# The norms' variances and shifts one element at a time, with a scalar pointer

## The chip, the cores and the metric

The kernel runs on one core of a Trainium2 chip. The metric is the device time of one execution in microseconds, the median of the runs taken. Five engines work side by side, each with its own list of instructions, and meet through semaphores: TensorE (PE, the matmuls), VectorE (DVE), ScalarE (ACT, activations), GpSimd (POOL) and SyncE (SP, which issues the DMAs).

## What is computed

The input is x, 8 x 512 rows of 256 floats. Two blocks follow each other, each added to its input:

```python
def _layernorm(x, axis=-1, eps=1e-05):
    m = jnp.mean(x, axis=axis, keepdims=True)
    v = jnp.var(x, axis=axis, keepdims=True)
    return (x - m) / jnp.sqrt(v + eps)
...
x = x + attn_ref(_layernorm(x))   # norm, linear attention (F = 64), norm, 256 -> 1024 -> 256 with GELU
x = x + ffn_ref(_layernorm(x))    # ternary weights, 256 -> 1024, GELU, norm over 1024, 1024 -> 256
```

`attn_ref` normalises its input, forms Q = elu(..)+1 and K = elu(..)+1 (64 features) and V (256), runs causal linear attention along the sequence with a denominator, applies the output projection and a residual, normalises again and runs an MLP with exact GELU and a residual. `ffn_ref` multiplies by weights rounded to -1, 0, 1 about their mean absolute value, applies GELU, a norm with weight and bias over 1024, and a second ternary matmul. Everything is float32.

## The kernel before

The 4096 rows are worked in 8 groups g of 512 rows, each as T = 4 tiles t of 128 rows on the partitions; h = 0, 1 names a half, two tiles. Float32 products are made as three passes of a faster type on a high and a low part (`split3`, L178 to L180), so that each operand is first written as `_hi` by ACT and then as `_lo` by DVE (`lo_part`, L806).

The order of the work is written out by hand. Each engine has a function `first` for the start, a function `step(g)` for g = 1 to 5, and `last`; they call the pieces of work of several groups in turn, so that a step holds the MLPs of group g, the end of group g-1 and the attention of group g+1. An engine does its list in order; `wait_ge` on a semaphore holds it, and everything behind it on that engine, until the count is reached.

There are four norms. For each of them DVE takes statistics (`bn_stats`), writes one element to a scratch tile (`fence`, L770), aggregates to mean and variance per row (`bn_aggr` to `mv`, L772), writes `ve` = variance + eps (`variance`, L779), POOL raises it to -1/2 (`rs`, L1043, and L1036 for the first norm), and DVE writes `sh` = -mean x rs (`shift`, L784). Norms 1 to 3 (n = 0, 1, 2) are then applied by ACT as scale and bias of an activation (`normalise`, L503): norm 1 of x gives u (for Q, K, V) and n1, the residual; norm 2 gives z, which PE transposes (L186) and ACT and DVE split into z2T; norm 3 gives z3T in the same way. Norm 4 is applied after the last matmul: `correct` (L930) adds csum x sh, and `output` (L947) multiplies by rs.

The first norm is two norms in one: `_layernorm` and then the attention's own one. Its `ve` and `sh` have two rows of four elements (L794, L795, L802); norms 2 to 4 work on the two elements of a half. Where each of them stands among DVE's pieces of work can be read in `first`, `step` and `last`.

POOL adds, besides its powers: n1 + bo (`n1o`, L1061), x + f2b (`xpb`, L1073), y + xa (`xs`, L1080) and y + cpj (`y_cpj`, L1090), each as two tensor_tensor operations of 128x512, one for each half.

The functions that the change touches, and what calls them:

Of the kernel before, what the change touches and what calls it, by code (L numbers as in the profile page):

```python
# [7 lines left out]
ALU = mybir.AluOpType  # L8
# [4 lines left out]
LN_EPS = 1e-5  # L13
# [6 lines left out]
def build(nc, x, wqk_d, wv_d, wo_d, f1_d, f2_d, fc_d, pj_d, vec_d, rows_d, out):  # L20
    G, N, D = x.shape
    FQ = 64
    T = N // P
# [11 lines left out]
    with ExitStack() as ctx:  # L35
        def sb(name, shape, dt=F32):
            return ctx.enter_context(nc.sbuf_tensor(name, shape, dt))

        def sem(name):
            return ctx.enter_context(nc.semaphore(name))  # L40
# [64 lines left out]
        mv = [sb(f"mv{n}", [P, T, 2]) for n in range(4)]  # L105
        ve = [sb("ve0", [P, 2, T])] + [sb(f"ve{n}", [P, T]) for n in (1, 2, 3)]
        rs = [sb("rs0", [P, 2, T])] + [sb(f"rs{n}", [P, T]) for n in (1, 2, 3)]
        sh = [sb("sh0", [P, 2, T])] + [sb(f"sh{n}", [P, T]) for n in (1, 2, 3)]
# [25 lines left out]
        s = {n: sem(n) for n in names}  # L134
# [309 lines left out]
        def _(act):  # L444
# [56 lines left out]
            def normalise(dst, src, n, t, row, ready):  # L501
                bias, scale = [a[n][:, row, t:t + 1] if n == 0 else a[n][:, t:t + 1] for a in (sh, rs)]
                act.activation(dst[:, t, :], src[:, t, :], ACT.Identity, bias=bias, scale=scale).then_inc(s[ready], 1)  # L503

            def u_norm(g, h):
                act.wait_ge(s["ln1_sh"], 2 * g + 1)
                if g:
                    act.wait_ge(s["tu_done"], 2 * (g - 1) + h + 1)
                for t in (2 * h, 2 * h + 1):
                    normalise(u, x_sb, 0, t, 1, "u_ready")  # L510

            def n1(g):
                act.wait_ge(s["ln1_sh"], 2 * g + 2)
                if g:
                    act.wait_ge(s["z2_ready"], 4 * g)
                    act.wait_ge(s["xs_ready"], 2 * g)
                else:
                    act.wait_ge(s["bvo_done"], 1)
                for t in range(T):
                    normalise(xa, x_sb, 0, t, 0, "n1_ready")  # L520
# [42 lines left out]
                act.activation(v[0][:, 2 * h:2 * h + 2, 0:D], by_k(bank_a[h]), ACT.Copy).then_inc(s["v_hi"], 1)  # L563

            def z2_norm(g, h):
                act.wait_ge(s["ln2_sh"], 2 * g + h + 1)
                if g:
                    act.wait_ge(s["tz3_done"], 2 * (g - 1) + h + 1)
                for t in (2 * h, 2 * h + 1):
                    normalise(z, xa, 1, t, 0, "z2_ready")  # L570
# [18 lines left out]
                act.activation(hr[0][:, (8 * g + m) % RH, :], bank_f[m % 2][:], ACT.Copy).then_inc(s["h_hi"], 1)  # L589

            def z3_norm(g, h):
                act.wait_ge(s["ln3_sh"], 2 * g + h + 1)
                act.wait_ge(s["tz2_done"], 2 * g + h + 1)
                for t in (2 * h, 2 * h + 1):
                    normalise(z, y, 2, t, 0, "z3_ready")
# [26 lines left out]
            def first():  # L622

                ln3_hi(); u_norm(0, 0); wqk_hi(); u_norm(0, 1); u_hi(0, 0); u_hi(0, 1); wvo_hi(); wf1_hi(0)
                wf1_hi(1); qk_exp(0); wf1_hi(2); qk_hi(0); eps_split(); wf2_hi(0); n1(0); ae_hi(0); ad_hi(0)
                wf2_hi(1); wf1_hi(3); af_hi(0); wf2_hi(2); v_hi(0, 0); wf2_hi(3); v_hi(0, 1); abs_part(0)
                abs_part(1); abs_part(2); abs_part(3); z2_norm(0, 0); z2_norm(0, 1); z2_hi(0, 0); z2_hi(0, 1)
                u_norm(1, 0); gelu(0, 0); h_hi(0, 0); gelu(0, 1); u_hi(1, 0); u_norm(1, 1); h_hi(0, 1); gelu(0, 2)
                u_hi(1, 1); n1(1); h_hi(0, 2); gelu(0, 3); h_hi(0, 3); qk_exp(1); gelu(0, 4); h_hi(0, 4); qk_hi(1)
                rows(); gelu(0, 5); h_hi(0, 5); gelu(0, 6); h_hi(0, 6); af_hi(1); gelu(0, 7); h_hi(0, 7)  # L630
                spread_copy(); ad_hi(1); ae_hi(1); v_hi(1, 0); v_hi(1, 1); z3_norm(0, 0); z3_norm(0, 1); z3_hi(0, 0)
                z3_hi(0, 1); gelu3(0, 0, 0); gelu3(0, 0, 1); gelu3(0, 1, 0); z2_norm(1, 0); gelu3(0, 1, 1)
                gelu3(0, 2, 0); g_hi(0, 0, 0); gelu3(0, 2, 1); g_hi(0, 0, 1); z2_norm(1, 1); g_hi(0, 0, 2)
                gelu3(0, 3, 0); z2_hi(1, 0); z2_hi(1, 1); g_hi(0, 0, 3); gelu3(0, 3, 1); u_norm(2, 0)
# [34 lines left out]
        def _(dve):  # L669
# [97 lines left out]
            def aggregate(n, ts, bn_count, mv_count):  # L767

                dve.wait_ge(s[f"ln{n + 1}_bn"], bn_count)
                dve.tensor_scalar(fence[:], neg_half[:, 0:1], 1.0, None, ALU.mult)  # L770
                for t in ts:
                    dve.bn_aggr(mv[n][:, t, :], bn[n][:, t, :]).then_inc(s[f"ln{n + 1}_mv"], 1)  # L772
                dve.wait_ge(s[f"ln{n + 1}_mv"], mv_count)

            def variance(n, g, h):

                if g:
                    dve.wait_ge(s[f"ln{n + 1}_rs"], 2 * (g - 1) + h + 1)
                dve.tensor_scalar(ve[n][:, 2 * h:2 * h + 2], mv[n][:, 2 * h:2 * h + 2, 1], 1.0, LN_EPS,  # L779
                                  ALU.mult, ALU.add).then_inc(s[f"ln{n + 1}_ve"], 1)  # L780

            def shift(n, g, h):
                dve.wait_ge(s[f"ln{n + 1}_rs"], 2 * g + h + 1)
                dve.scalar_tensor_tensor(sh[n][:, 2 * h:2 * h + 2], mv[n][:, 2 * h:2 * h + 2, 0], -1.0,  # L784
                                         rs[n][:, 2 * h:2 * h + 2], ALU.mult, ALU.mult).then_inc(s[f"ln{n + 1}_sh"], 1)

            def ln1_stats(g):
                for t in range(T):
                    dve.wait_ge(s[f"x_loaded{t // 2}"], 16 * g + 16)
                    dve.bn_stats(bn[0][:, t, :], x_sb[:, t, :]).then_inc(s["ln1_bn"], 1)  # L790
                aggregate(0, range(T), 4 * g + 4, 4 * g + 4)
                if g:
                    dve.wait_ge(s["ln1_rs"], g)
                dve.tensor_scalar(ve[0][:, 0, :], mv[0][:, :, 1], 1.0, LN_EPS, ALU.mult, ALU.add).then_inc(s["ln1_ve"], 1)  # L794
                dve.tensor_scalar(ve[0][:, 1, :], mv[0][:, :, 1], 1.0 + LN_EPS, LN_EPS * LN_EPS,  # L795
                                  ALU.mult, ALU.add).then_inc(s["ln1_ve"], 1)

            def ln1_shift(g):

                dve.wait_ge(s["ln1_rs"], g + 1)  # L800
                for row in (1, 0):
                    dve.scalar_tensor_tensor(sh[0][:, row, :], mv[0][:, :, 0], -1.0, rs[0][:, row, :],  # L802
                                             ALU.mult, ALU.mult).then_inc(s["ln1_sh"], 1)

            def lo_part(dst, b, hi, ready):
                dve.tensor_tensor(dst, b, hi.bitcast(F32), ALU.subtract).then_inc(s[ready], 1)  # L806
# [70 lines left out]
            def ln2_var(g, h):  # L877
                aggregate(1, (2 * h, 2 * h + 1), 4 * g + 2 * h + 2, 4 * g + 2 * h + 2)
                variance(1, g, h)
# [20 lines left out]
            def ln3_stats(g, h):  # L900
                dve.wait_ge(s["y_ready"], 2 * g + h + 1)
                for t in (2 * h, 2 * h + 1):
                    dve.bn_stats(bn[2][:, t, :], y[:, t, :]).then_inc(s["ln3_bn"], 1)
                aggregate(2, (2 * h, 2 * h + 1), 4 * g + 2 * h + 2, 4 * g + 2 * h + 2)
                variance(2, g, h)
# [18 lines left out]
            def correct(g, h):  # L924

                shift(3, g, h)
                dve.wait_ge(s["ln4_sh"], 2 * g + h + 1)
                dve.wait_ge(s["yc_ready"], 2 * g + h + 1)
                for t in (2 * h, 2 * h + 1):
                    dve.scalar_tensor_tensor(yc[:, t, :], csum_b, sh[3][:, t:t + 1], yc[:, t, :],  # L930
                                             ALU.mult, ALU.add).then_inc(s["corrected"], 1)
# [76 lines left out]
        def _(pool):  # L1008
# [18 lines left out]
                return row.unsqueeze(1).to_broadcast([P, 2, D])  # L1027

            def ln1_rstd(g):
                pool.wait_ge(s["ln1_ve"], 2 * g + 2)  # L1030
                if g:
                    pool.wait_ge(s["u_ready"], 4 * g)
                    pool.wait_ge(s["n1_ready"], 4 * g)
                else:
                    pool.wait_ge(s["sums_w"], 1)
                pool.tensor_tensor(rs[0][:].rearrange("p c t -> p (c t)"), ve[0][:].rearrange("p c t -> p (c t)"),  # L1036
                                   neg_half[:], ALU.pow).then_inc(s["ln1_rs"], 1)

            def rstd(n, g, h, freed, count):
                pool.wait_ge(s[f"ln{n + 1}_ve"], 2 * g + h + 1)  # L1040
                if g:
                    pool.wait_ge(s[freed], count)
                pool.tensor_tensor(rs[n][:, 2 * h:2 * h + 2], ve[n][:, 2 * h:2 * h + 2], neg_half[:, 0:2],  # L1043
                                   ALU.pow).then_inc(s[f"ln{n + 1}_rs"], 1)
# [113 lines left out]
```

## Time and profile before

| | us |
|---|---|
| median of 3 runs | 482.81 (481.68 to 483.86) |
| the profiled execution | 483.59 |
| its span | 481.8 |
| mean granted TensorE clock, share of full | 0.971 |
| PE busy, share of the span | 455.1, 94% |
| DVE busy | 385.3, 80% |
| ACT busy | 324.1, 67% |
| POOL busy | 134.4, 28% |

The span goes from the first to the last instruction of the program; the execution's own time is 1.8 us longer. Busy time is the union of an engine's instructions. A group of instructions is shown by line, engine, operation, the tile that it writes and those it reads, with its count, its busy time, the mean of one in ns, and the idle time of the engine ahead of it with what ended that idle time. Instructions of one engine overlap in the records, so that the next can start before the one ahead has ended; what an instruction costs its engine is read from start to start.

### The profile page before, as it was taken

To read this page: it belongs to the slowest core of one execution; us is meant where nothing else is said; L and a number is where in the kernel's file an instruction comes from. 1 tells how busy PE (TensorE), PEld (TensorE's weight loads), DVE (VectorE), ACT (ScalarE), POOL (GpSimd) and SP (SyncE) were. 2 spreads that over 40 slices of the span, in tenths; PEclk is the share of its full clock that TensorE was granted. 3 is DMA by queue.
4 is the path that set the end of the run, shared out by engine and by line. 5 is a ranking of instruction groups with operands and counts; after the bars stand their busy time and mean duration, and the time that the engine had idled before them with its cause. 6 is when DMAs were issued, how large, how long until landed. Compare 5 with 4: busy or idle time off the path is not lost.

```text
span 481.8 us, 8668 instructions
## 1 busy us (share of the span) xinstructions
PE 455.1 (94%) x3010; PEld 409.9 (85%) x3010; DVE 385.3 (80%) x1011; ACT 324.1 (67%) x611; POOL 134.4 (28%) x132
## 2 busy tenths in 40 slices
PE   4786998999999999999999999999999989999796
PEld 4785888889988899889988899889989889889686
DVE  4686969886997969976997969976999688874767
ACT  3776864797558783897558783897469854783263
POOL 2173305310372023600371023600361021501400
PEclk9875999999999999999999999999999999999889
DMA  8330000100020000100010000100020000000001
GB/s 252 131 114 19 1 0 1 44 23 2 0 68 1 24 0 24 45 22 1 3 65 1 23 1 24 45 22 1 2 66 2 24 0 23 1 23 2 22 0 45
DMA packets 10042, 14.06 MB, mean 29 GB/s; under 512 B 784, under 2 KB 9104, under 8 KB 9488
## 3 DMA queue, kind: packets, MB, share of 16 engines
q1 hardware_dynamic: 10000, 13.52, 8.3%
q8 instruction: 24, 0.39, 0.4%
q14 instruction: 18, 0.15, 0.1%
HBM read 9.32 MB, written 4.19 MB: 28 GB/s over the span
## 4 chain that ended last, share of the span: by engine, by line
PE 64%; DVE 17%; issue 11%; ACT 2%; POOL 2%; DMA 1%; SPq 0%; DVEq 0%; POOLq 0%; ACTq 0%
PE bank_p L393 8%; PE bank_y L178 6%; PE bank_f L363 6%; PE bank_y L179 6%; PE bank_y L180 6%; PE bank_f L178 6%; PE bank_f L179 5%; PE bank_f L180 5%; PE bank_y L377 4%; PE bank_a L186 3%; DVE sh L784 2%; DVE bn L918 2%; PE bank_a L178 2%; PE bank_a L180 2%; PE bank_a L179 2%
## 5 line engine op out<-in xcount | busy, mean ns | idle before, releaser
L1043 POOL TENSOR_TENSOR rs<-ve,neg_half 128x2 f32<-128x2 f32 x48 | 33.6, 702 | 245.9 <-DVE ve L779 245.9
L178 PE MATMUL bank_y<-wf_hi,h_hi 128*128 128x256 f32 x256 | 72.4, 283 | 1.5 <-DVE h_lo L806 1.5
L179 PE MATMUL bank_y<-wf_lo,h_hi 128*128 128x256 f32 x256 | 71.5, 279 | 0.0
L180 PE MATMUL bank_y<-wf_hi,h_lo 128*128 128x256 f32 x256 | 71.5, 279 | 0.0
L806 DVE TENSOR_TENSOR h_lo<-bank_f,h_hi 128x512 fp32r<-128x512 f32 x64 | 43.9, 686 | 28.4 <-ACT h_hi L589 28.2
L393 PE MATMUL bank_p<-wpj_t,g_hi 128*128 128x256 f32 x256 | 65.1, 289 | 0.4 <-DVE g_lo L938 0.2
L393 PE MATMUL bank_p<-wpj_t,g_lo 128*128 128x256 f32 x256 | 62.6, 280 | 0.0
L938 DVE SCALAR_TENSOR_TENSOR g_lo<-bank_y,vec,g_hi 128x256 fp32r<-128x256 f32 x128 | 54.9, 475 | 6.5 <-ACT g_hi L619 6.3
L619 ACT ACTIVATE g_hi<-bank_y,vec 128x256 fp32r<-128x256 f32 x128 | 53.4, 483 | 8.6 <-PE bank_y L377 7.4
L610 ACT ACTIVATE h<-bank_f 128x512 f32<-128x512 f32 x64 | 38.1, 601 | 25.7 <-PE bank_f L363 25.3
L363 PE MATMUL bank_f<-wfc_t,z3T_hi 128*128 128x512 f32 x128 | 54.5, 426 | 0.2 <-ACT h L610 0.2
L583 ACT ACTIVATE bank_f<-bank_f,f_bias 128x512 f32<-128x512 f32 x64 | 42.0, 662 | 18.6 <-PE bank_f L180 17.7
L178 PE MATMUL bank_f<-z2T_hi,wf_hi 128*128 128x512 f32 x128 | 52.2, 408 | 1.4 <-DVE z2T_lo L806 1.4
L363 PE MATMUL bank_f<-wfc_t,z3T_lo 128*128 128x512 f32 x128 | 51.5, 402 | 0.0
L178 PEld LDWEIGHTS bank_y<-wf_hi,h_hi 128*128 128x128 f32 x256 | 48.1, 188 | 3.7 <-DVE h_lo L806 1.7
L179 PE MATMUL bank_f<-z2T_lo,wf_hi 128*128 128x512 f32 x128 | 51.2, 400 | 0.0
L180 PE MATMUL bank_f<-z2T_hi,wf_lo 128*128 128x512 f32 x128 | 51.1, 399 | 0.0
L393 PEld LDWEIGHTS bank_p<-wpj_t,g_hi 128*128 128x128 f32 x256 | 48.1, 188 | 1.3 <-issue 0.4
L179 PEld LDWEIGHTS bank_y<-wf_lo,h_hi 128*128 128x128 f32 x256 | 48.0, 187 | 1.1
L393 PEld LDWEIGHTS bank_p<-wpj_t,g_lo 128*128 128x128 f32 x256 | 48.2, 188 | 0.5
L180 PEld LDWEIGHTS bank_y<-wf_hi,h_lo 128*128 128x128 f32 x256 | 48.0, 188 | 0.0
L918 DVE BATCH_NORM_STATS2 bn<-h 128x6 f32<-128x512 f32 x64 | 41.2, 683 | 2.9 <-ACT h L610 2.5
(168 smaller groups left out, 1154.2 us busy)
## 6 DMA issues: line engine op xcount, KB each, us to landing
x_sb<-in_x SPq DMA_DIRECT2D x16, 256.0 KB, 2.8
out<-y_yc SPq DMA_DIRECT2D x16, 256.0 KB, 2.1
h<-in_f SPq DMA_DIRECT2D x1, 1024.0 KB, 8.0
y_yc<-in_f SPq DMA_DIRECT2D x1, 1024.0 KB, 9.9
h<-in_fc SPq DMA_DIRECT2D x1, 1024.0 KB, 11.9
h<-in_pj SPq DMA_DIRECT2D x1, 1024.0 KB, 4.7
z<-in_wv SPq DMA_DIRECT2D x1, 256.0 KB, 3.5
z<-in_wo SPq DMA_DIRECT2D x1, 256.0 KB, 3.7
```

What stands on the lines that cost most here:

```text
L178: pe.matmul(ps, w[0], r[0], start=start, stop=False, skip_group_check=skip)
L179: pe.matmul(ps, w[0], r[1], start=False, stop=False, skip_group_check=skip)
L180: return pe.matmul(ps, w[1], r[0], start=False, stop=stop, skip_group_check=skip)
L363: mm = pe.matmul(bank_f[c][:], z3T[part][:, k, t * P:(t + 1) * P], wfc[:, k, c * 512:(c + 1) * 512], start=(k == 0 and part == 0), stop=(k ...
L393: mm = pe.matmul(bank_p[:, t * D:(t + 1) * D], gr[part][:, (8 * g + 4 * h + q) % RG, i, t * P:(t + 1) * P], wpj[:, m, :], start=(m == 0 an ...
L583: act.activation(bank_f[m % 2][:], bank_f[m % 2][:], ACT.Gelu, bias=f1_bias[:, m:m + 1]).then_inc(s["h_gelu"], 1)
L610: act.activation(h3[:, t, c * 512:(c + 1) * 512], bank_f[c][:], ACT.Gelu).then_inc(s["h3_ready"], 1)
L619: act.activation(gr[0][:, n % RG, i, :], bank_y[q % 2][:, i * D:(i + 1) * D], ACT.Copy, scale=ln3w_c[:, m:m + 1]).then_inc(s["g_hi"], 1)
L806: dve.tensor_tensor(dst, b, hi.bitcast(F32), ALU.subtract).then_inc(s[ready], 1)
L918: dve.bn_stats(bn[3][:, t, 6 * c:6 * c + 6], h3[:, t, c * 512:(c + 1) * 512]).then_inc(s["ln4_bn"], 1)
L938: dve.scalar_tensor_tensor(gr[1][:, n % RG, i, :], bank_y[q % 2][:, i * D:(i + 1) * D], ln3w_c[:, m:m + 1], gr[0][:, n % RG, i, :].bitcast ...
L1043: pool.tensor_tensor(rs[n][:, 2 * h:2 * h + 2], ve[n][:, 2 * h:2 * h + 2], neg_half[:, 0:2], ALU.pow).then_inc(s[f"ln{n + 1}_rs"], 1)
```

## The change

Each `ve` and `sh` of 2 or 4 elements is written by as many instructions of one element. `ve` stays a tensor_scalar with two constants. `sh` was a scalar_tensor_tensor with two tensor inputs, mean and rs, and becomes a tensor_scalar with one tensor input, the mean, and rs as a pointer scalar. Every instruction adds one to its semaphore, and the counts that ACT, POOL and DVE wait for follow: for norms 2 to 4 from 2g+h+1 to 4g+2h+2, for norm 1 from 2g+2 to 8g+8, and from 2g+1 to 8g+4 where u waits for the first row. POOL's powers keep their sizes. All calls stand where they stood.

```diff
@@ u_norm, n1 (ACT)
-                act.wait_ge(s["ln1_sh"], 2 * g + 1)
+                act.wait_ge(s["ln1_sh"], 8 * g + 4)
...
-                act.wait_ge(s["ln1_sh"], 2 * g + 2)
+                act.wait_ge(s["ln1_sh"], 8 * g + 8)
@@ z2_norm, z3_norm (ACT)
-                act.wait_ge(s["ln2_sh"], 2 * g + h + 1)
+                act.wait_ge(s["ln2_sh"], 4 * g + 2 * h + 2)
...
-                act.wait_ge(s["ln3_sh"], 2 * g + h + 1)
+                act.wait_ge(s["ln3_sh"], 4 * g + 2 * h + 2)
@@ variance, shift (DVE)
-                dve.tensor_scalar(ve[n][:, 2 * h:2 * h + 2], mv[n][:, 2 * h:2 * h + 2, 1], 1.0, LN_EPS,
-                                  ALU.mult, ALU.add).then_inc(s[f"ln{n + 1}_ve"], 1)
+                for t in (2 * h, 2 * h + 1):
+                    dve.tensor_scalar(ve[n][:, t:t + 1], mv[n][:, t, 1:2], 1.0, LN_EPS,
+                                      ALU.mult, ALU.add).then_inc(s[f"ln{n + 1}_ve"], 1)
...
-                dve.scalar_tensor_tensor(sh[n][:, 2 * h:2 * h + 2], mv[n][:, 2 * h:2 * h + 2, 0], -1.0,
-                                         rs[n][:, 2 * h:2 * h + 2], ALU.mult, ALU.mult).then_inc(s[f"ln{n + 1}_sh"], 1)
+                for t in (2 * h, 2 * h + 1):
+                    dve.tensor_scalar(sh[n][:, t:t + 1], mv[n][:, t, 0:1], rs[n][:, t:t + 1], -1.0,
+                                      ALU.mult, ALU.mult).then_inc(s[f"ln{n + 1}_sh"], 1)
@@ ln1_stats, ln1_shift (DVE)
-                dve.tensor_scalar(ve[0][:, 0, :], mv[0][:, :, 1], 1.0, LN_EPS, ALU.mult, ALU.add).then_inc(s["ln1_ve"], 1)
-                dve.tensor_scalar(ve[0][:, 1, :], mv[0][:, :, 1], 1.0 + LN_EPS, LN_EPS * LN_EPS,
-                                  ALU.mult, ALU.add).then_inc(s["ln1_ve"], 1)
+                for row, (scale, shift) in enumerate(((1.0, LN_EPS), (1.0 + LN_EPS, LN_EPS * LN_EPS))):
+                    for t in range(T):
+                        dve.tensor_scalar(ve[0][:, row, t:t + 1], mv[0][:, t, 1:2], scale, shift,
+                                          ALU.mult, ALU.add).then_inc(s["ln1_ve"], 1)
...
                 for row in (1, 0):
-                    dve.scalar_tensor_tensor(sh[0][:, row, :], mv[0][:, :, 0], -1.0, rs[0][:, row, :],
-                                             ALU.mult, ALU.mult).then_inc(s["ln1_sh"], 1)
+                    for t in range(T):
+                        dve.tensor_scalar(sh[0][:, row, t:t + 1], mv[0][:, t, 0:1], rs[0][:, row, t:t + 1], -1.0,
+                                          ALU.mult, ALU.mult).then_inc(s["ln1_sh"], 1)
@@ correct (DVE), ln1_rstd and rstd (POOL): counts alone
-                dve.wait_ge(s["ln4_sh"], 2 * g + h + 1)
+                dve.wait_ge(s["ln4_sh"], 4 * g + 2 * h + 2)
...
-                pool.wait_ge(s["ln1_ve"], 2 * g + 2)
+                pool.wait_ge(s["ln1_ve"], 8 * g + 8)
...
-                pool.wait_ge(s[f"ln{n + 1}_ve"], 2 * g + h + 1)
+                pool.wait_ge(s[f"ln{n + 1}_ve"], 4 * g + 2 * h + 2)
```

## Rows read from the trace of the kernel before

**Rows 1.** The page, part 1: busy us (share of the span) x instructions.

```profile
PE 455.1 (94%) x3010; PEld 409.9 (85%) x3010; DVE 385.3 (80%) x1011; ACT 324.1 (67%) x611; POOL 134.4 (28%) x132
```

**Rows 2.** Waits of PE: who waited for whom, us in total, times, longest.

```profile
PE bank_f L186 <- ACT z L503: 3.9, 3, 2.1
PE bank_a L186 <- ACT z L503: 3.8, 2, 3.2
PE bank_y L377 <- DVE g_lo L938: 1.7, 5, 0.6
PE bank_y L178 <- DVE h_lo L806: 1.5, 1, 1.5
PE bank_f L178 <- DVE z2T_lo L806: 1.4, 1, 1.4
...
PE bank_a L307 <- DVE v_lo L806: 0.8, 2, 0.5
```

**Rows 3.** Single lines: count, ns shortest/median/longest, first and last start, form.

```profile
L784 DVE SCALAR_TENSOR_TENSOR sh<-mv,rs x48: 143/160/1244, 37.1 to 477.1; 128x2 f32<-128x2 f32 x48
...
L779 DVE TENSOR_SCALAR ve<-mv x48: 157/169/1193, 35.1 to 476.1; 128x2 f32<-128x2 f32 x48
...
L770 DVE TENSOR_SCALAR fence<-neg_half x72: 134/153/155, 5.1 to 475.0; 128x1 f32<-128x1 f32 x72
...
L930 DVE SCALAR_TENSOR_TENSOR y_yc<-pj_rows_b,sh,y_yc x32: 471/482/1484, 97.5 to 477.7; 128x256 f32<-128x256 f32 x32
```

**Rows 4.** Timeline of a step: start us, us, engine, line [idle <- releaser].

```profile
192.44 2.54 POOL L1073 TENSOR_TENSOR y_yc<-x_sb,rows_b 128x512 f32<-128x512 f32 x2
...
192.57 1.19 DVE L779 TENSOR_SCALAR ve<-mv 128x2 f32<-128x2 f32 x1
...
199.77 0.63 PE L377 MATMUL bank_y<-ident,h 128*128 128x128 f32 x4 [0.26 <-DVE g_lo L938]
...
202.30 0.17 DVE L794 TENSOR_SCALAR ve<-mv 128x4 f32<-128x4 f32 x1
202.37 0.16 DVE L795 TENSOR_SCALAR ve<-mv 128x4 f32<-128x4 f32 x1
```

**Rows 5.** DVE's groups by form: xcount | busy us, mean ns | idle before.

```profile
L938 DVE SCALAR_TENSOR_TENSOR g_lo<-bank_y,vec,g_hi 128x256 fp32r<-128x256 f32 x128 | 54.9, 475 | 6.5 <-ACT g_hi L619 6.3
...
L790 DVE BATCH_NORM_STATS2 bn<-x_sb 128x6 f32<-128x256 f32 x32 | 11.2, 407 | 1.3 <-DMA x_sb<-in_x 1.3
```

**Rows 6.** Timeline, group 0's second norm, DVE and ACT.

```profile
38.03 1.22 DVE L784 SCALAR_TENSOR_TENSOR sh<-mv,rs 128x2 f32<-128x2 f32 x1 [0.75 <-POOL rs L1043]
...
39.29 1.09 ACT L503 ACTIVATE z<-xa,sh,rs 128x256 f32<-128x256 f32 x2 [0.88 <-DVE sh L784]
```

**Rows 7.** Timeline, group 0's third norm, DVE and PE.

```profile
79.38 1.24 DVE L784 SCALAR_TENSOR_TENSOR sh<-mv,rs 128x2 f32<-128x2 f32 x1 [0.15 <-POOL rs L1043]
...
81.79 0.66 PE L186 MATMUL bank_f<-ident,z 128*128 128x128 f32 x4 [0.60 <-ACT z L503]
```

**Rows 8.** Timeline, group 1's f1 and what stands ahead of it on DVE.

```profile
95.92 0.23 DVE L802 SCALAR_TENSOR_TENSOR sh<-mv,rs 128x4 f32<-128x4 f32 x2
96.06 0.68 DVE L806 TENSOR_TENSOR z2T_lo<-bank_a,z2T_hi 128x512 fp32r<-128x512 f32 x1
...
97.37 0.39 PE L178 MATMUL bank_f<-z2T_hi,wf_hi 128*128 128x512 f32 x1
```

**Rows 9.** Timeline of DVE, two of the corrections.

```profile
230.37 0.67 DVE L784 SCALAR_TENSOR_TENSOR sh<-mv,rs 128x2 f32<-128x2 f32 x1
...
391.71 1.24 DVE L784 SCALAR_TENSOR_TENSOR sh<-mv,rs 128x2 f32<-128x2 f32 x1 [0.28 <-POOL rs L1043]
392.99 1.87 DVE L930 SCALAR_TENSOR_TENSOR y_yc<-pj_rows_b,sh,y_yc 128x256 f32<-128x256 f32 x2
```

**Rows 10.** Timeline, the last group's third norm, DVE and PE.

```profile
452.82 1.22 DVE L784 SCALAR_TENSOR_TENSOR sh<-mv,rs 128x2 f32<-128x2 f32 x1
...
455.21 1.12 PE L186 MATMUL bank_f<-ident,z 128*128 128x128 f32 x4 [1.13 <-ACT z L503]
```

## The prediction

> **What bounds the kernel now.** I read the page first: the tensor engine (PE) is busy 455.1 of 481.8 us [rows 1]. Then its waits: apart from the loading at the start, only short ones, and most of them are for results of the norms: 3.9 us (3 times) and 3.8 us (2 times) for a normalised z, 1.7 us (5 times) for g_lo, 1.5 for h_lo, 1.4 for z2T_lo, 0.8 for v_lo [rows 2]. So an edit on DVE changes the time only where one of these waits ends, or where its delay outgrows the lead that DVE has over PE.
>
> Then the lines that change. The two-element `ve` (L779) takes 169 ns in the median but up to 1193, the two-element `sh` (L784) 160 but up to 1244 [rows 3]. The long ones lie under a GpSimd (POOL) tensor_tensor: `ve` at 192.57 begins 0.13 us after POOL's first L1073, and lasts 1.19, to that one's end [rows 4]. I went through the 96 in the timeline so: all that are over 240 ns, 6 of `ve` and 22 of `sh`, lie under such an operation. The additions at L930 (two SBUF tensors) wait too, 1484 against 482 [rows 3].
>
> **Does the new form wait?** The new `ve` is a tensor_scalar of one element with constants. The trace has it: the fence of L770, 72 times, 134 to 155 ns [rows 3]; 25 of them lie wholly under POOL operations. So I let `ve` wait for nothing. The new `sh`, one element with a pointer scalar, isn't there. Bounds: no wait at all (the fence), or one like today's, up to 1.24 us. I take no wait: it has one tensor input, as the fence has.
>
> The Trainium skill ("SBUF — State Buffer", the section on the two separate sides) says that VectorE and GpSimd lock one port pair for a whole instruction, VectorE when it runs in a two-port mode or has two SBUF inputs. [...]
>
> **What an instruction costs.** DVE instructions overlap, so the price is the distance between starts. Two `ve` in a row start 0.07 apart (202.30, 202.37, then 202.44 for the next), so each added `ve` costs 0.07 to 0.08 [rows 4]. A pointer costs more: four stats of 256 columns without one last 407 each, g_lo with one 475 [rows 5]; and in the timeline these start 0.33 and 0.395 apart. So a pointer op of one element is 0.07+0.065 = 0.135 (bounds 0.07 and 0.20, one and three such steps), and its result is 0.06 later. Per group of 512 rows `ve` goes from 8 to 20 instructions, `sh` too. Over eight groups: 96 x 0.077 = 7.4 us for `ve`; 160 x 0.135 - 64 x 0.07 = 17.1 us for `sh`; 24.5 us added to a DVE that is busy 385. What leaves is the waiting: about 5 us of `ve`, and of `sh` some 14 us, of which the part ahead of L930 only moves on to L930. DVE gets slightly more work in all; its place decides. No DMA, no POOL or ACT instruction is added; POOL and ACT wait for higher counts.
>
> **The places, in order of time** (negative is a gain).
> - Start, 5 to 12 us: six more `ve` (0.46) and three more `sh` (0.4) ahead of u. The first matmuls on wv and wo (to 10.8) cover it; the second transpose has 1.05 us of lead. 0; without cover 0.9.
> - Group 0, 38 to 43: `sh` at 38.03 waits 1.22, and z at 39.29 with it [rows 6]. After: the first half's `ve`, `sh` come 0.26 later, ACT runs on without its idle 0.88, so the second half is 0.67 earlier; ln1's six `ve` (0.46) lie ahead of z2T_lo but the start is 0.7 earlier. f1 0.55 earlier; the GELU table load, bound to u's norm, leaves 0.2 to 0.5 of it. -0.4.
> - Group 0's ln3: `sh` at 79.38 waits 1.24 and z for it, PE idle 0.60 at 81.79 [rows 7]. z comes 0.74 earlier, but v_lo, behind two `ve` and a `sh` pair, 0.35 later, and PE waits for v_lo there. -0.6+0.35 = -0.25.
> - In the first group only, ln1's `sh` (95.92) stands ahead of z2T_lo (96.06): six more, and each dearer, 8 x 0.135 - 2 x 0.07 = 0.94, and a `ve`. f1, which needs z2T_lo's end (96.74), starts at 97.37 [rows 8], z2T_lo's lead is 0.63. +0.35.
> - Steps g = 1 to 5: PE idles once, 0.60, then four times 0.26 to 0.28 (199.77) for g_lo [rows 2, 4]. DVE is busy without a break before it. Between 184 and 198.8 a step loses the wait of `ve` at 192.57 (1.10 to 0.155: -0.95), that of ln3's `sh` (0.88 to 0.27, of which 0.24 gets past the next wait for z3T_hi), and gains two or three `ve` and one `sh` pair inside that: g_lo about 1 us earlier. The gap goes: -(0.60+0.26+0.26+0.27+0.28) = -1.65. Late next: h3 from ACT, which follows PE, so nothing more is won.
> - The same steps behind it: ln2's second `sh` +0.2, ln1's `ve` +0.46, ln1's `sh` +0.94, ln4's `sh` +0.2. z2T_lo waits for its ACT half in any case; g_lo at 206.09 comes 1.1 later with 1.57 us of lead. 0; if pointers cost 0.20, 0.3 per step.
> - ln4's correction (230.37): the wait of 0.67 goes from `sh` to L930, whose second half waits for POOL's second addition either way: h_lo at 232.87 or 0.1 earlier [rows 9]. 0. Its twin at 391.71, 1.24 and then L930 1.87 us, ends the wait of 1.47 at h_lo [rows 2, 9]: the first L930 now waits 1.0 in place of `sh`, POOL's second addition goes in between, the second L930 waits for that. -0.1. If both L930 pass ahead of it, -1.2.
> - End: `sh` at 452.82 waits 1.22, z at 454.07 for it, PE idles 1.13 at 455.21 [rows 10]. First half 0.35 later (two `ve`, a `sh` pair), second one bound by ACT, which ends its first pair at 453.5: -0.55. Behind it DVE leads by 0.15 to 0.65 us only, and two `ve`, a `sh` pair stand in its way: +0.15.
>
> Sum: 0-0.4-0.25+0.35-1.65-0.1-0.55+0.15 = -2.45 us. The profiled execution took 483.6 (span 481.8), so 481.1 and a span of 479.4; it lay 0.8 above the median 482.8, from which I take it off: 480.4.
>
> **Rivals.**
> - The gaps before g_lo stay: another input of the same chain, g_hi or the fourth attn_out, is as late as `ve`. For it: PE's idle is 0.26, so little that any second cause fills it; against: DVE has no idle there and g_hi leads by 1 us. -2.45+1.65 = -0.8: 482.0.
> - Both L930 pass ahead of POOL's second addition. For it: a waiting DVE operation does get in between two of POOL's (the `sh` of 391.71 ended at 392.95 with POOL's first addition, not its second [rows 9]). Against: between the two L930 it is POOL that waits, and by the same rule gets in. -1.1 more: 479.3.
> - Slower: the pointer makes `sh` wait as now, and the second of the pair waits for POOL's second operation. POOL works in pairs of 1.25 to 1.3 us (2.54 for two L1073 [rows 4]). It decides wherever a `sh` meets the first of a pair and PE waits for z: 38.03 and 79.38, +1.2 each on top of today's and without the gains there (+0.65), then 0.3 at each of six corrections, 0.35 at the end with its gain of 0.55 gone: 2.4+0.65+1.8+0.35+0.55 = 5.75, on -2.45: +3.3, 486.1. Against: one tensor input; `sh` under POOL's pow (L1043) is short, but so are all others there, so that no row decides. [...]
> - The change doesn't do what it says: `ve`'s one-element form is already in the trace, so for it I see no case.
>
> **Numbers.** The forecast's own case 0.50 (479.5 to 481.4, from a pointer step of 0.07 or 0.20 and a table load that keeps all of -0.4); gaps stay 0.20; L930 both pass 0.18; slower 0.12, of which 0.02 for the strict reading. A measurement of this kernel tells 0.5%, 2.4 us, from no change; the forecast sits on that line. So faster 0.24+0.17 = 0.41, within 0.48 (half of the first, nearly all of the second), slower 0.11. The range 478.8 to 483.0 leaves out most of the slower case.
>
> **What would show it.** Right: no `ve` over 0.18 us; `sh` around 0.21 us and 0.135 apart, even under POOL; L930 waiting at both places; no idle of PE for g_lo near 146, 200, 254, 308 and 362; z3's wait near 455 shorter by half. Wrong: `sh` over 0.3 us under a POOL addition (then slower), new waits of PE for z2T_lo or g_lo in each step (then DVE's added 3 us per group outgrow its lead), or the 0.26 still there.

## The result

| | before | after |
|---|---|---|
| median | 483.29 us (481.68 to 483.92, 6 runs) | 478.83 us (477.68 to 478.93, 6 runs) |
| profiled execution | 483.59 us | 477.68 us |
| its span | 481.8 us | 476.0 us |
| granted TensorE clock | 0.971 | 0.978 |

The ratio is 0.9906, 95% interval [0.9887, 0.9925]: 4.5 us faster (3.6 to 5.5). 480.4 us with a range of 478.8 to 483.0 was forecast. The time lies at the low edge of the range, and as a share of the kernel before just past it: 0.9906, where 478.8 of the 482.81 that the forecast started from is 0.9917. The gain is nearly twice the 2.45 us worked out, and clearly over the 0.5% on whose line the forecast sat. The granted clock doesn't make the difference: at a mean of 0.978 the kernel before took 482.6 to 483.4 us in the runs below, the changed one 477.7 to 478.9.

The two profiled executions stand 5.8 us apart in span, of which about 0.9 is there at 32 us, ahead of the first norm 2. That is no effect of the change: the same 0.9 stands there in the profile of a kernel (f1 below) in which norms 1 and 2 are old. Another 1.0 is there from 32 to 50 us, where the clock differs too (see "Group 0's norm 2" below). So places are compared behind it.

The page of the kernel after, part 1, as in [rows 1]:

```profile
PE 451.1 (95%) x3010; PEld 408.0 (86%) x3010; DVE 387.9 (81%) x1203; ACT 324.2 (68%) x611; POOL 135.6 (28%) x132
```

DVE has 192 instructions more and 2.6 us more busy time, PE is busy 4.0 us less with the same 3010 matmuls (some waits stand in the records as a longer matmul, as the one at 233.60 below). Its waits after:

```profile
PE bank_a L186 <- ACT z L503: 3.4, 1, 3.4
PE bank_f L186 <- ACT z L503: 2.4, 1, 2.4
...
PE bank_a L307 <- DVE v_lo L810: 1.5, 3, 0.5
...
PE bank_y L178 <- DVE h_lo L810: 1.3, 1, 1.3
```

Against [rows 2], z fell from 7.7 to 5.8 us, the 1.7 for g_lo is gone, v_lo rose from 0.8 to 1.5. With h_lo that makes 3.1 us less; what more was won was in no wait of before. The single lines after, to be read beside [rows 3]:

```profile
L780 DVE TENSOR_SCALAR ve<-mv x96: 143/145/156, 33.9 to 470.3; 128x1 f32<-128x1 f32 x96
...
L786 DVE TENSOR_SCALAR sh<-mv,rs x96: 200/204/215, 36.3 to 471.3; 128x1 f32<-128x1 f32 x96
...
L934 DVE SCALAR_TENSOR_TENSOR y_yc<-pj_rows_b,sh,y_yc x32: 472/486/1518, 95.5 to 472.0; 128x256 f32<-128x256 f32 x32
```

Neither form waits any more: the longest of 96 is 156 and 215 ns, where two elements took up to 1193 and 1244. In runs of equal instructions two `ve` start 0.06 to 0.07 apart and two `sh` 0.12 (forecast 0.07 to 0.08 and 0.135). Only the additions (two SBUF tensors) still wait, up to 1518.

Some names of the kernel: f1 and f2 of a group are the two float32 matmuls of the first block's MLP (L178 to L180, into bank_f and bank_y), fc and proj (L363, L393) the two ternary ones of the second block, and tr the transposes between these (L377), for which g_lo has to be done. Below, f1 to f4 are also the labels of four runs.

Where PE's lead over the kernel before is won, from the start of the same matmul in both timelines (after minus before, as 195.94 against the 199.77 of [rows 4]; counted from 50 us on):

| place | forecast | measured |
|---|---|---|
| group 0, norm 3 (81.79) | -0.25 | -0.55 |
| f1 of group 1 (97.37) | +0.35 | +0.23 |
| g_lo in steps 1 to 5 | -1.65 | -2.50 (-0.76, then four times -0.43 to -0.44) |
| behind g_lo in the steps | 0 | +0.16, once |
| f2's last part, five steps and the last | -0.1 | -1.08 (six times -0.17 to -0.20) |
| end | -0.40 | -0.21 |
| in no one place | | -0.05 |
| sum | -2.05 | -4.00 |

A step after, DVE with POOL and PE:

```profile
183.98 0.32 DVE L786 TENSOR_SCALAR sh<-mv,rs 128x1 f32<-128x1 f32 x2
184.22 0.87 DVE L951 SCALAR_TENSOR_TENSOR y_yc<-bank_p,rs,y_yc 128x256 f32<-128x256 f32 x2
...
188.59 2.52 POOL L1077 TENSOR_TENSOR y_yc<-x_sb,rows_b 128x512 f32<-128x512 f32 x2
188.99 0.21 DVE L780 TENSOR_SCALAR ve<-mv 128x1 f32<-128x1 f32 x2
...
192.42 2.53 POOL L1084 TENSOR_TENSOR y_yc<-y_yc,xa 128x512 f32<-128x512 f32 x2
...
194.15 0.34 DVE L786 TENSOR_SCALAR sh<-mv,rs 128x1 f32<-128x1 f32 x2
194.40 1.68 DVE L942 SCALAR_TENSOR_TENSOR g_lo<-bank_y,vec,g_hi 128x256 fp32r<-128x256 f32 x4
...
195.94 0.60 PE L377 MATMUL bank_y<-ident,h 128*128 128x128 f32 x4
```

The pair of `ve` at 188.99 lies wholly under POOL's L1077 and the `sh` at 194.15 under its L1084, and both pass; the tr behind has no idle.

### The profile page after: what moved, and what is told of

Read it like the earlier page. It is cut to its first block, busy times and chain, and to the rows that moved or that the text cites. A ratio compares the mean times of both kernels' runs of the same rounds, so it can differ in the third digit from the quotient of the medians.

```text
span 476.0 us, 8860 instructions
## 1 busy us (share of the span) xinstructions
PE 451.1 (95%) x3010; PEld 408.0 (86%) x3010; DVE 387.9 (81%) x1203; ACT 324.2 (68%) x611; POOL 135.6 (28%) x132
## 4 chain that ended last, share of the span: by engine, by line
PE 74%; DVE 11%; issue 8%; POOL 2%; ACT 1%; DMA 1%; SPq 0%; DVEq 0%; POOLq 0%; ACTq 0%
PE bank_f L363 10%; PE bank_p L393 9%; PE bank_y L178 6%; PE bank_y L179 6%; PE bank_y L180 6%; PE bank_f L178 5%; PE bank_f L179 5%; PE bank_f L180 5%; PE bank_y L377 4%; PE bank_a L178 4%; PE bank_a L180 3%; PE bank_a L179 3%; PE bank_a L186 2%; DVE g_lo L942 1%; PE bank_f L186 1%
## 5 line engine op out<-in xcount | busy, mean ns | idle before, releaser
L178 PE MATMUL bank_y<-wf_hi,h_hi 128*128 128x256 f32 x256 | 71.9, 281 | 1.3 <-DVE h_lo L810 1.3
L180 PE MATMUL bank_y<-wf_hi,h_lo 128*128 128x256 f32 x256 | 71.5, 279 | 0.0
L393 PE MATMUL bank_p<-wpj_t,g_hi 128*128 128x256 f32 x256 | 65.1, 289 | 0.4 <-DVE g_lo L942 0.2
L393 PE MATMUL bank_p<-wpj_t,g_lo 128*128 128x256 f32 x256 | 62.6, 280 | 0.0
L363 PE MATMUL bank_f<-wfc_t,z3T_hi 128*128 128x512 f32 x128 | 54.7, 427 | 0.4 <-DVE z3T_lo L810 0.3
L178 PE MATMUL bank_f<-z2T_hi,wf_hi 128*128 128x512 f32 x128 | 52.1, 407 | 1.9 <-DVE z2T_lo L810 1.4
L363 PE MATMUL bank_f<-wfc_t,z3T_lo 128*128 128x512 f32 x128 | 51.7, 404 | 0.0
L180 PE MATMUL bank_f<-z2T_hi,wf_lo 128*128 128x512 f32 x128 | 51.0, 399 | 0.0
L178 PEld LDWEIGHTS bank_y<-wf_hi,h_hi 128*128 128x128 f32 x256 | 48.1, 188 | 2.9 <-DVE h_lo L810 1.5
L393 PEld LDWEIGHTS bank_p<-wpj_t,g_hi 128*128 128x128 f32 x256 | 48.1, 188 | 1.3 <-DVE g_lo L942 0.4
L393 PEld LDWEIGHTS bank_p<-wpj_t,g_lo 128*128 128x128 f32 x256 | 48.2, 188 | 0.5
L180 PEld LDWEIGHTS bank_y<-wf_hi,h_lo 128*128 128x128 f32 x256 | 48.0, 188 | 0.0
```

The costliest lines, as they stand in the source:

```text
L178: pe.matmul(ps, w[0], r[0], start=start, stop=False, skip_group_check=skip)
L180: return pe.matmul(ps, w[1], r[0], start=False, stop=stop, skip_group_check=skip)
L363: mm = pe.matmul(bank_f[c][:], z3T[part][:, k, t * P:(t + 1) * P], wfc[:, k, c * 512:(c + 1) * 512], start=(k == 0 and part == 0), stop=(k ...
L393: mm = pe.matmul(bank_p[:, t * D:(t + 1) * D], gr[part][:, (8 * g + 4 * h + q) % RG, i, t * P:(t + 1) * P], wpj[:, m, :], start=(m == 0 an ...
```

## The experiments

Each was timed beside the kernel before on the same chip, in three batches of four; "before" was 482.9, 483.2 and 482.8 us in them. Gains in us are worked out from the ratio, which goes by means and can differ by some tenths from the difference of the medians. Two constants say for which norms the new form is used, `VE1` for `ve` and `SH1` for `sh` (norm 1 is 0, norm 4 is 3); the counts that are waited for follow. In the kernels that mix the forms (e1 to e4, f1 to f4, g2, g4) the lines of PE and ACT lie 2 higher than before, DVE's from lo_part on (L828) and POOL's 22 (`correct` L952, g_lo L960, output L969, xs L1102); `ve` is L783 new and L786 old, `sh` L793 new and L796 old.

**e1: only `ve` new.**

```diff
+VE1 = (0, 1, 2, 3)
+SH1 = ()
```

> Only the variances (ve) of all four norms are written one element at a time; the shifts (sh) keep the old form. Theory A (each term at its own place: what is won is PE's waits behind DVE operations that wait for POOL): the gaps at g_lo in the five steps go (0.43 us each between starts, 0.76 in the first, together 2.5, of which ve carries nearly all), the waits at f2's last part, at group 0's z and at the last z stay, since they hang on sh. 483.3-2.3 = 481.0 us, and no ve over 0.18 us. Rival B (the gain is TensorE's granted clock in the first 50 us, not the norms): the same as the changed kernel or as before, by chance, 479 or 483. Rival C (nearly all comes from sh, as the longer list of waits, 14 us against 5, suggests): 482.8.

Measured 483.09 us (482.1 to 484.32), ratio 1.0008 [0.9995, 1.0022]: nothing, as its rival C said. My reason for the largest term fell here. DVE and POOL in a step:

```profile
191.39 0.21 DVE L783 TENSOR_SCALAR ve<-mv 128x1 f32<-128x1 f32 x2
...
195.11 2.53 POOL L1102 TENSOR_TENSOR y_yc<-y_yc,xa 128x512 f32<-128x512 f32 x2
196.42 1.25 DVE L796 SCALAR_TENSOR_TENSOR sh<-mv,rs 128x2 f32<-128x2 f32 x1
197.59 1.65 DVE L960 SCALAR_TENSOR_TENSOR g_lo<-bank_y,vec,g_hi 128x256 fp32r<-128x256 f32 x4
...
198.59 0.63 PE L379 MATMUL bank_y<-ident,h 128*128 128x128 f32 x4 [0.32 <-DVE g_lo L960]
```

`ve` waits no more, DVE comes 1 us earlier to norm 2's `sh`, and that one now takes 1.25 us (0.32 before), to the end of POOL's second addition at 197.64. g_lo starts where it did. The wait only moved to the next operation that needs POOL to be done. That holds for steps 2 to 5. In step 1, where norm 2's `sh` doesn't meet POOL's second addition, this profile has the whole gap of 0.76 gone; steps 2 to 4 lose 0.05 to 0.07 each, and where the rest goes is not shown.

**e2: only `sh` new.**

```diff
+VE1 = ()
+SH1 = (0, 1, 2, 3)
```

> Only the shifts (sh) are written one element at a time with a pointer scalar; the variances keep the old form. Theory A: ve at the fourth attn_out still waits 1.1 us, so that the gap at g_lo stays but for some 0.2 us a step (sh of norm 3, 1.0 in all); f2's last part is won (6 times 0.18 = 1.1), and group 0 and the last z (about 1.2). Together -3.0 at most, 480.5 to 481.5 us. Rival B: 479 or 483. Rival C: 479.2, nearly the whole gain.

Measured 477.94 us (477.56 to 478.83), ratio 0.9896 [0.9878, 0.9914]: the whole gain, rival C again. The idle ahead of g_lo is gone in steps 2 to 5 although `ve` (0.90 at 189.55) still waits. That left a question: which `sh`, and how.

**e3: norm 1 old, norms 2 to 4 new.**

```diff
+VE1 = (1, 2, 3)
+SH1 = (1, 2, 3)
```

> The change without norm 1: its ve and sh keep the form of four elements, norms 2 to 4 are as in the changed kernel. Norm 1's operations never lie under a POOL addition, so they have nothing to win, and the twelve added ones (0.9 to 1.1 us of DVE per group) go. Theory A: only the places where they are on the way count, f1 of group 1 (0.3) and perhaps 0.2 at the start: 0.3 to 0.5 faster than the changed kernel's 478.8, 478.4. Rival D (DVE's sheer amount of work sets the pace): 8 us less DVE work give 1.5 us or more, 477.3.

Measured 477.78 us (476.59 to 478.06), ratio 0.9885 [0.9867, 0.9904]. By the ratios norm 1's 96 added instructions cost 1.0 us, but the two intervals overlap, so that neither nothing nor 2 us is ruled out. One place shows in the profiles: from its start to the tr behind, f1 of group 1 loses 0.23 in the changed kernel and wins 0.16 here, 0.4 in all.

**e4: one element, but two tensor inputs.**

```diff
-                    dve.tensor_scalar(sh[n][:, t:t + 1], mv[n][:, t, 0:1], rs[n][:, t:t + 1], -1.0,
-                                      ALU.mult, ALU.mult).then_inc(s[f"ln{n + 1}_sh"], 1)
+                    dve.scalar_tensor_tensor(sh[n][:, t:t + 1], mv[n][:, t, 0:1], -1.0, rs[n][:, t:t + 1],
+                                             ALU.mult, ALU.mult).then_inc(s[f"ln{n + 1}_sh"], 1)
```

> As the changed kernel, but sh is a scalar_tensor_tensor of one element with two tensor inputs, mean and rs, in place of the tensor_scalar with a pointer; number of instructions and counts are the same. Theory A with the two inputs as what makes it wait: sh over 0.24 us wherever it meets a POOL addition, and the second of a pair waits for POOL's second addition as well, up to 1.3 us: +1.2 at each of two places in group 0, 0.3 at each of six corrections, on top of what ve alone gives (481.0): 485 us, in a range of 483 to 486. Rival E (one element is enough, whatever the inputs): no sh over 0.2 us, and a little faster than the changed kernel since no pointer is read: 478.5.

Measured 484.36 us (483.19 to 485.85), ratio 1.0029 [1.0016, 1.0042], slower than before. Its `sh` ahead of g_lo, and the wait of PE:

```profile
197.56 1.32 DVE L793 SCALAR_TENSOR_TENSOR sh<-mv,rs 128x1 f32<-128x1 f32 x2
```

```profile
PE bank_y L379 <- DVE g_lo L960: 2.5, 5, 0.7
```

So one element with two tensor inputs waits as two elements did: for `sh` one element is not enough, the second tensor has to go. Whether the pointer alone would free an `sh` of two elements was not run; `ve`, a tensor_scalar without a second tensor, does wait with two.

**f1: only norm 3's `sh` new. f2: only norm 4's. f3: only norm 2's.**

```diff
+VE1 = ()
+SH1 = (2,)
```

The same with `SH1 = (3,)` in f2 and `(1,)` in f3.

> Only norm 3's shift is in the new form (one element, pointer); every ve and the shifts of norms 1, 2 and 4 are as before. Theory A (norm 3's shift stands ahead of the previous group's output; output, its store and then POOL's additions follow it, so that this one shift sets when POOL's additions to y end, and with them all waits ahead of g_lo): the idle of PE before g_lo (0.26 to 0.28 in steps 2 to 5) is gone, 2.2 us in five steps, PE 0.77 earlier at the first group's z3 and 0.4 net in the last group's: -3.4, 479.5 us where the kernel before takes 482.9. h_lo of f2's last part keeps its place. Rival B (the gap needs also norm 2's shift, which stands right before g_lo and waits under POOL's second addition): idle before g_lo stays at 0.2 or more, -1.2, 481.7.

Measured 479.84 us (478.01 to 480.14), ratio 0.9917 [0.9899, 0.9935]: -4.0 of the 4.5 to 5.4 us that all of them give. As theory A said, PE wins 0.42 to 0.44 at g_lo in each of steps 2 to 5, 0.50 in step 1, and f2's last part keeps its place.

> Only norm 4's shift is in the new form. Theory A (each of its waits moved h_lo of the last part of f2, a delay that the records don't show as idle): PE 0.17 to 0.20 earlier in each of five steps and 0.3 in the last, nothing else: -1.2, 481.7 us against 482.9. The pair of additions behind it (L930 of the kernel before) waits for POOL in its place for the first or the second. Rival B (the gain there in the run with all shifts new came from another norm's shift, norm 1's, which stands just ahead on DVE): nothing, 482.9.

Measured 481.85 us (480.91 to 483.54), ratio 0.9973 [0.9961, 0.9986]: -1.3, where 1.2 was expected. PE wins 0.17 to 0.22 at h_lo of each group's f2 and nothing at g_lo. The correction of 230.37 [rows 9], in the kernel before, with what stands around it:

```profile
229.73 2.54 POOL L1061 TENSOR_TENSOR xa<-xa,bo_b 128x512 f32<-128x512 f32 x2 [5.63 <-ACT xa L503]
...
231.07 1.87 DVE L930 SCALAR_TENSOR_TENSOR y_yc<-pj_rows_b,sh,y_yc 128x256 f32<-128x256 f32 x2
232.87 0.68 DVE L806 TENSOR_TENSOR h_lo<-bank_f,h_hi 128x512 fp32r<-128x512 f32 x1
...
233.42 0.28 PE L180 MATMUL bank_y<-wf_hi,h_lo 128*128 128x256 f32 x1
233.60 0.39 PE L178 MATMUL bank_y<-wf_hi,h_hi 128*128 128x256 f32 x1
233.83 0.28 PE L179 MATMUL bank_y<-wf_lo,h_hi 128*128 128x256 f32 x1
```

and in f2:

```profile
229.21 2.73 POOL L1083 TENSOR_TENSOR xa<-xa,bo_b 128x512 f32<-128x512 f32 x2 [5.63 <-ACT xa L505]
229.85 0.33 DVE L793 TENSOR_SCALAR sh<-mv,rs 128x1 f32<-128x1 f32 x2
230.21 2.02 DVE L952 SCALAR_TENSOR_TENSOR y_yc<-pj_rows_b,sh,y_yc 128x256 f32<-128x256 f32 x2
232.15 0.68 DVE L828 TENSOR_TENSOR h_lo<-bank_f,h_hi 128x512 fp32r<-128x512 f32 x1
```

Before, `sh` gets in between POOL's two additions and both L930 come behind the second one (229.73+2.54 = 232.27). In f2 the first addition of the correction gets in between (POOL's pair takes 2.73 for 2.54) and only one is left behind it (229.21+2.73 = 231.94). From the `sh` to h_lo it is 2.50 us before and 2.30 in f2. And PE does wait there: h_lo ends at 233.55, the matmul at 233.60 begins 0.18 after the one ahead of it and the next 0.23 after that, where all the others stand 0.12 apart: 0.17 us lost with no idle recorded.

> Only norm 2's shift is in the new form. Theory A: 0.6 to 0.7 us in group 0 (z2 of the second half), in the steps the shift right before g_lo no longer waits 0.3 us under POOL's second addition but costs one more start of 0.12, so 0 to -0.15 a step: -0.7 to -1.4, 482.2 to 481.5 us. Rival B (norm 2's shift is what fills the gap before g_lo): idle before g_lo gone as with all shifts new, -0.43 a step, -2.8, 480.1.

Measured 482.73 us (481.28 to 483.83), ratio 0.9979 [0.9967, 0.9991]: -1.0, within the 0.7 to 1.4 expected. It doesn't touch the gap in steps 2 to 5. Its profile has PE 0.77 earlier at the z of group 0's second half (40.44), the place expected, but only 0.23 of that is left at 50 us; it has -0.34 at step 1's g_lo and gives it back by step 5. So where the -1.0 comes from stays open.

**f4: `sh` of norms 2 to 4 new, all else old.**

```diff
+VE1 = ()
+SH1 = (1, 2, 3)
```

> The shifts of norms 2 to 4 are new, norm 1's shift and every ve as before: the candidate for the best mix. Theory A (ve is worth nothing once POOL's additions come earlier; norm 1's 16 shifts cost 0.35 us once, ahead of f1 of group 1, and fill DVE): 477.5 us, 0.4 less than all shifts new and 1.2 less than the whole change with its added ve instructions. Rival B (norm 1's form costs nothing measurable and ve's neither): 477.8 to 478.0, the same as both.

Measured 478.04 us (477.46 to 478.19), ratio 0.9888 [0.9873, 0.9904]: the same as the whole change within the intervals, with 48 added instructions in place of 192. The three alone sum to -6.3 (each known to 0.6 to 0.9), together they give -5.4.

**How norm 3's `sh` reaches g_lo.** The chain that ended last, in the kernel before, has it (start, us, what; here in step 5):

```profile
348.97 0.95 DVE sh L784
350.74 2.09 DMA out<-y_yc
352.99 1.27 POOL y_yc L1090
...
358.10 2.51 POOL y_yc L1080 x2
```

The same in the timeline of step 2 of the kernel before:

```profile
187.19 0.96 DVE L784 SCALAR_TENSOR_TENSOR sh<-mv,rs 128x2 f32<-128x2 f32 x1
188.07 0.86 DVE L947 SCALAR_TENSOR_TENSOR y_yc<-bank_p,rs,y_yc 128x256 f32<-128x256 f32 x2
...
191.18 1.30 POOL L1090 TENSOR_TENSOR y_yc<-y_yc,pj_rows_b 128x512 f32<-128x512 f32 x1 [3.05 <-DMA out<-y_yc]
...
196.27 2.54 POOL L1080 TENSOR_TENSOR y_yc<-y_yc,xa 128x512 f32<-128x512 f32 x2
198.51 0.32 DVE L784 SCALAR_TENSOR_TENSOR sh<-mv,rs 128x2 f32<-128x2 f32 x1
198.76 1.65 DVE L938 SCALAR_TENSOR_TENSOR g_lo<-bank_y,vec,g_hi 128x256 fp32r<-128x256 f32 x4
```

`output` of the group before stands right behind that `sh`. Its rows are stored, POOL's `y_cpj` waits for the store (its buffer is free only then), and seven POOL operations follow each other without a break. POOL's last one ends at 198.81, norm 2's `sh` with it, and g_lo is next. So an `sh` that takes 0.96 us at 187 (0.16 without a wait) sets g_lo at 199. From `output` to g_lo in this step it is 10.69 us here and in f3, 10.70 in e1 and e2, 10.71 in f1. If this is right, moving `output` alone must move g_lo:

**g1: the kernel before, with `output` one call earlier.**

```diff
-                v_lo(g + 1, 1); ln3_shift(g, 1); output(g - 1, 1); ln2_stats(g + 1, 0); attn_out(g + 1, 1)
+                v_lo(g + 1, 1); output(g - 1, 1); ln3_shift(g, 1); ln2_stats(g + 1, 0); attn_out(g + 1, 1)
```

> The kernel before with every ve and sh in its old form; in the five steps output(g-1,1) is called one place earlier, ahead of norm 3's second shift instead of behind it. Theory A (the chain output, its store, POOL's additions, the end of xs's second one, norm 2's shift, g_lo is what sets the gap before g_lo; DVE's own amount of work ahead of g_lo doesn't matter): output starts 0.88 us earlier against PE, POOL's additions too, and PE's idle before g_lo goes with no change of form: -0.5 and four times -0.43, 480.8 us where the kernel before takes 483.0. Rival B (DVE has too much to do ahead of g_lo, which this order leaves as it is): 483.0 and the idle of 0.26 stays.

Measured 481.07 us (480.34 to 481.76), ratio 0.9966 [0.9951, 0.998]: -1.65 with every form old. PE wins 0.49 and four times 0.42 to 0.44 at g_lo, as in f1, and its waits for g_lo at tr are gone but for 0.11 in step 1. From output to g_lo it is again 10.71:

```profile
186.68 0.88 DVE L947 SCALAR_TENSOR_TENSOR y_yc<-bank_p,rs,y_yc 128x256 f32<-128x256 f32 x2 [0.29 <-PE bank_p L393]
...
194.90 2.54 POOL L1080 TENSOR_TENSOR y_yc<-y_yc,xa 128x512 f32<-128x512 f32 x2
197.13 0.33 DVE L784 SCALAR_TENSOR_TENSOR sh<-mv,rs 128x2 f32<-128x2 f32 x1
197.39 1.65 DVE L938 SCALAR_TENSOR_TENSOR g_lo<-bank_y,vec,g_hi 128x256 fp32r<-128x256 f32 x4
```

**g2: f1 with `output` later. g3: the whole change with `output` later.**

```diff
-                v_lo(g + 1, 1); ln3_shift(g, 1); output(g - 1, 1); ln2_stats(g + 1, 0); attn_out(g + 1, 1)
+                v_lo(g + 1, 1); ln3_shift(g, 1); ln2_stats(g + 1, 0); attn_out(g + 1, 1); output(g - 1, 1)
```

> Norm 3's shift alone in the new form, as in f1, and in the five steps output(g-1,1) behind ln2_stats(g+1,0) and attn_out(g+1,1), 1.0 us later. Theory A: POOL's additions end 1.0 us later than in f1, norm 2's old shift waits for the end of the second one and g_lo with it: of the 1.0 some 0.17 was lead, 0.8 us lost at each of five g_lo, 4.1 on f1's 479.8: 483.9 us, as slow as the kernel before or slower, with DVE's instructions the same as f1's. Rival B: as f1, 479.8.

Measured 484.94 us (484.43 to 486.04), ratio 1.005 [1.0035, 1.0065]: f1's gain is gone and more, with f1's instructions, 5.1 us on f1 where 4.1 was expected. I had taken 1.0 us for the move; `output` starts 1.70 behind the `sh` of 186.57 where it was 0.26 in f1, so it moved 1.44. PE's wait for g_lo:

```profile
PE bank_y L379 <- DVE g_lo L960: 5.5, 5, 1.2
```

```profile
186.57 0.33 DVE L793 TENSOR_SCALAR sh<-mv,rs 128x1 f32<-128x1 f32 x2
188.27 0.87 DVE L969 SCALAR_TENSOR_TENSOR y_yc<-bank_p,rs,y_yc 128x256 f32<-128x256 f32 x2
...
196.47 2.53 POOL L1102 TENSOR_TENSOR y_yc<-y_yc,xa 128x512 f32<-128x512 f32 x2
198.34 0.68 DVE L796 SCALAR_TENSOR_TENSOR sh<-mv,rs 128x2 f32<-128x2 f32 x1
198.94 1.65 DVE L960 SCALAR_TENSOR_TENSOR g_lo<-bank_y,vec,g_hi 128x256 fp32r<-128x256 f32 x4
```

> The whole change, and the same late output as in g2. Theory A: neither ve nor sh waits for POOL now, so that POOL's additions may end 1.0 us later at no cost: 478.8 us as the whole change, no idle before g_lo. Rival C (g_lo itself or another operation there waits for POOL too, or z3 is late): 0.4 to 0.8 in each of five steps, 481 to 483.

Measured 478.5 us (477.94 to 478.61), ratio 0.991 [0.9896, 0.9924]: the same as the change. POOL ends late, at 197.18, and g_lo no longer cares:

```profile
194.64 2.54 POOL L1084 TENSOR_TENSOR y_yc<-y_yc,xa 128x512 f32<-128x512 f32 x2
195.01 0.34 DVE L786 TENSOR_SCALAR sh<-mv,rs 128x1 f32<-128x1 f32 x2
195.26 1.65 DVE L942 SCALAR_TENSOR_TENSOR g_lo<-bank_y,vec,g_hi 128x256 fp32r<-128x256 f32 x4
```

From output to g_lo it is 8.83 us here. Two things tie g_lo to POOL, `ve` and norm 2's `sh`: with one of them new (e1, e2, f3) it stays 10.69 to 10.70, with both new it is 10.18, and 8.83 when POOL comes late.

**g4: f4 with `output` early,** the edit of g1.

> Shifts of norms 2 to 4 new, norm 1 and every ve old, and the early output of g1: the candidate for the fastest. Theory A: steps 2 to 5 have no idle left to win, step 1 had 0.8 in the kernel with those shifts alone and loses it: 477.5 us against 478.0. Rival B: nothing more than 478.0, or 0.2 a step lost where norm 3's second shift comes later behind output.

Measured 478.63 us (477.48 to 479.19), ratio 0.9913 [0.9898, 0.9929]: nothing on top of f4. The 477.5 of theory A counted on step 1, but PE's wait for g_lo there stays:

```profile
PE bank_y L379 <- DVE g_lo L960: 0.8, 1, 0.8
```

In both kernels that tr starts 0.2 us later against the one ahead of it than in the kernel before; with `ve` new (e1, e3, the change) this wait is gone. So step 1 is the one place where the new `ve` shows a gain in the profiles. Of the versions run none is faster than the change by more than the intervals allow (e3 0.9885, f4 0.9888, e2 0.9896, the change 0.9906).

## Why the prediction came out wrong

- **"Does the new form wait?" No: right**, and it is the base of everything. All 192 one-element `ve` and `sh` of norms 2 to 4 are short, and under POOL too. For `sh` it was an assumption; the trace after and e4 bear it out. (Of the 72 fences of the kernel before 23 lie wholly under POOL operations, not 25, and 17 of these under an addition, the kind that made the others wait.) The Trainium skill ("SBUF — State Buffer", Who interferes with whom) says that a VectorE instruction with at most one SBUF input outside the two-port modes does not contend with GpSimd, and one with two SBUF inputs does where the GpSimd instruction reads SBUF; e4 against the change agrees, 1.32 against 0.34 us for a pair in the same place. So the rs that comes as a pointer doesn't count as such an input here. The case to which 0.02 was given, a one-element `ve` that waits as well, did not come: 156 ns at most.
- **"What an instruction costs": right**, a little high (0.12 for 0.135, 0.06 to 0.07 for 0.07 to 0.08). The added 24.5 us cost next to nothing in the steps, as said (0.16 once, in step 5).
- **The steps' g_lo, -1.65: right in sign, wrong in cause and size.** I gave 0.95 of the 1 us to `ve` at 192.57. e1 took exactly that away and moved g_lo in none of steps 2 to 5 (in step 1 it did, by 0.76). I had added up DVE's work ahead of g_lo as if only DVE set it; but the next wait on POOL ends at a time that POOL sets, and POOL's time was set by `output`, behind norm 3's `sh` (f1, g1, g2). It came out with the right sign by luck, because the change frees that `sh` as well. In size: I took the recorded idle (0.26) for the loss. The matmul ahead of the tr of 199.77 began 0.66 before it where 0.23 is usual, so 0.43 was lost, and 0.43 to 0.44 was won.
- **Corrections, 0 for the steps: wrong, the largest miss, 1.0 us** (-1.08 for the six of them, forecast 0 for five and -0.1 for the last). "The second half waits for POOL's second addition either way: h_lo at 232.87 or 0.1 earlier" was the right mechanism; it is 0.20 earlier. The failure was to call it free because no idle of PE stands there. A matmul of 0.39 among those of 0.28 and a start 0.18 behind the last one were the sign. f2 measures it alone: -1.3 us.
- **Group 0's norm 3, -0.25: mis-sized**, -0.55: z gave 0.77 and 0.05, v_lo took 0.25 back (0.35 forecast); the loss of 0.60 was again the recorded idle.
- **f1 of group 1, +0.35: right in sign**, +0.23. **End, -0.40: too much**, -0.21: z3 gave 0.94, but its first half came 0.28 late and the fc matmuls behind took 0.45 back. Of this 0.19 stands ahead of the first of them, where the matmuls now wait 0.3 for z3T_lo, and 0.26 is the clock, which the forecast left out: PE idles over 2 us for the last z, the granted clock is at its lower level, 0.50, from 453.6 to 460.4 us before and from 448.0 to 454.8 after, and as PE starts the fc 6.2 us earlier but the clock comes back only 5.6 earlier, one more of them starts 0.43 behind the one ahead in place of 0.23, and the next 0.30.
- **Group 0's norm 2, -0.4: open.** From 32 to 50 us PE won 1.0 in the profile after, but 0.65 in f1's and lost 0.4 in f2's, with norm 2's forms old in both. The granted clock from 22 to 30 us was 0.50 in the profile before (the lower of the two levels, 1.2 GHz), 0.62 in the one after and 0.58 in e2's, so that one profile can't tell 0.4 there. The start did move as forecast: the z of the second half lets PE begin 0.53 earlier at 40.44 (0.55 was said). What is left of it depends on how long the clock then stays at 0.50, from 37.2 to 47.4 us in the profile before, from 38.4 to 45.2 in the one after. Of the profiles with the long stretch, the four with norm 2's new `sh` (e3, f3, f4, g4) won 0.05 to 0.09 from 32 to 50 us, the two others with the old one (f2, g2) lost 0.4; of those with the short stretch, the new one (the change, e2, g3) won 0.71 to 1.00 and the old one (e1, e4, f1, g1) 0.04 to 0.65. That points at a few tenths from the new form, and shows no more.
- **The rivals.** "Gaps stay" and "slower" fell (no idle ahead of g_lo in the change, no `sh` over 215 ns). "Both L930 pass" fell too: in f2 the first gets in between POOL's two additions, and the second waits, as the forecast's own case said.

## What to carry to other kernels

Before a wait is counted as a gain, look at the next one. When an operation waits for a resource that another engine holds, taking the wait away only helps if no later operation waits for the same holder; ask what sets the holder's own time, and look for it in the chain of waits (a short `sh`, a store and POOL's additions stood in it, eleven microseconds ahead of the gap). A one-call move of the work that starts the holder can win part of the same time with no new instruction (g1). And where the records show no idle, compare the distance between starts with its neighbours before an edit is called free.

## What was not expected of the hardware

- A DVE operation that waits for a POOL addition gets in between two of POOL's that follow each other, and POOL then waits for it: POOL's pair took 2.73 us in f2 in place of 2.54.
- One element with two SBUF tensors waits (up to 1324 ns in e4), one element with one tensor and a pointer never did (215 ns at most, with 51 of the 160 wholly under a POOL addition), and two elements of a tensor_scalar do (up to 1193 ns) where one element doesn't (156). Why the size matters in the last case no run here shows.
- The recorded idle of PE understates a loss: 0.26 for 0.43 us at g_lo, 0 for 0.17 us at h_lo.
